# A twelve-stage transformer stack on one core: the quantised layers' fronts made in the drain of the stage before them, weights and cleared operands a stage sooner

## The reference, cut to what matters

```
x = x + 0.5 * L0_ffn(ln(x));  x = x + L0_attn(ln(x));  x = x + 0.5 * L0_ffn(ln(x))
x = x + 0.5 * L1_ffn(ln(x));  x = x + L1_attn(ln(x));  x = x + 0.5 * L1_ffn(ln(x))
... the same with L2 and L3
```

```
xn = layernorm(x) * ln_gamma + ln_beta
gamma = max(abs(xn))                       # over all 4096 tokens
xq = clip(xn * 128 / gamma, -128+, 128-);  y = (xq @ w_q) * gamma * beta / 128
```

## Time and profile before

| | before |
|---|---|
| median of 3 runs | 4267.09 us (4266.0 to 4274.78) |
| the profiled execution | 4268.37 us |
| its span, first to last instruction | 4266.6 us |
| mean granted TensorE clock | 0.951 |
| PE busy | 3884.7 us (91%) |
| DVE busy | 3266.5 us (77%) |
| ACT busy | 3119.9 us (73%) |
| POOL busy | 1511.8 us (35%) |

### The profile page before, as it was taken

How to read it: one execution, slowest core, us unless ns; L and a number is a source line. 1 busy time by engine, 2 the same in 40 slices (tenths; PEclk the granted TensorE clock), 3 DMA queues, 4 the chain that set the end, 5 groups by cost and what they waited for, 6 DMA issues and landing times.

```text
span 4266.6 us, 58145 instructions
## 1 busy us (share of the span) xinstructions
PE 3884.7 (91%) x15924; PEld 2177.6 (51%) x15924; DVE 3266.5 (77%) x10600; ACT 3119.9 (73%) x5775; POOL 1511.8 (35%) x2843
## 2 busy tenths in 40 slices
PE   6799789999999999999999999998699669999976
PEld 4567634444444444444444444443366447777755
DVE  6877588888888888888888888886667766666668
ACT  3555369999999999999999999998243436666654
POOL 2331234444444444444444444443211114333320
PEclk8888799999999999999999999999799879999988
DMA  2122010000000000000100000000000001111100
GB/s 61 31 45 40 7 25 1 15 11 1 20 6 1 20 6 1 20 6 1 23 3 8 18 1 16 11 1 1 0 1 1 0 15 46 46 45 43 43 7 20
DMA packets 151990, 71.08 MB, mean 17 GB/s; under 512 B 109577, under 2 KB 142685, under 8 KB 151667
## 3 DMA queue, kind: packets, MB, share of 16 engines
q1 hardware_dynamic: 144738, 63.96, 5.8%
q10 hardware_dynamic: 6928, 3.41, 0.3%
HBM read 54.55 MB, written 12.80 MB: 16 GB/s over the span
## 4 chain that ended last, share of the span: by engine, by line
PE 59%; ACT 18%; DVE 14%; issue 6%; POOL 3%; DMA 0%; DVEq 0%; SPq 0%; ACTq 0%; POOLq 0%
PE bank L2093 16%; PE bank L2883 5%; PE bank L2108 5%; PE bank L2137 5%; ACT arena L2185 3%; PE bank L2916 3%; PE bank L2147 3%; ACT arena L2184 2%; ACT arena L2188 2%; ACT arena L2197 2%; DVE arena L2274 2%; ACT L2231 2%; PE bank L620 2%; PE bank L2943 1%; DVE arena L2297 1%
## 5 line engine op out<-in xcount | busy, mean ns | idle before, releaser
L2093 PE MATMUL bank<-arena 128*128 128x512 f32 x3072 | 1413.5, 593 | 3.9 <-DMA arena<-in_L_attn_Wv_dram 3.7
L2093 PEld LDWEIGHTS bank<-arena 128*128 128x128 f32 x3072 | 584.0, 190 | 739.9 <-issue 719.3
L2334 POOL TENSOR_SCALAR arena<-arena 128x256 f32<-128x256 f32 x1024 | 481.1, 481 | 1156.3 <-DVE arena L2267 1156.3
L2108 PE MATMUL bank<-arena 128*128 128x512 f32 x1024 | 524.5, 604 | 49.6 <-DVE arena L2297 49.6
L2256 DVE SCALAR_TENSOR_TENSOR arena<-arena 128x256 f32<-128x256 f32 x1024 | 393.7, 421 | 184.9 <-ACT arena L2185 176.5
L2297 DVE SCALAR_TENSOR_TENSOR arena<-arena 128x256 f32<-128x256 f32 x1024 | 491.7, 524 | 13.6 <-issue 13.6
L2274 DVE SCALAR_TENSOR_TENSOR arena<-bank,bv,arena 128x256 f32<-128x256 f32 x1024 | 444.7, 472 | 0.0
L2184 ACT ACTIVATE arena<-bank,bqk 128x512 f32<-128x512 f32 x512 | 348.5, 681 | 76.8 <-PE bank L2093 72.5
L2267 DVE SCALAR_TENSOR_TENSOR arena<-bank,bq,arena 128x512 f32<-128x512 f32 x512 | 384.1, 750 | 18.0
L2197 ACT ACTIVATE arena<-arena,const_table 128x512 f32<-128x512 f32 x512 | 374.7, 732 | 0.0
L2188 ACT ACTIVATE arena<-bank,bqk 128x512 f32<-128x512 f32 x512 | 354.3, 692 | 0.4 <-PE bank L2093 0.4
(11 more groups left out here) (396 smaller groups left out, 7056.3 us busy)
## 6 DMA issues: line engine op xcount, KB each, us to landing
arena<-packed_dram SPq DMA_DIRECT2D x96, 96.0 KB
arena<-packed_dram SPq DMA_DIRECT2D x32, 288.0 KB
arena<-diag_dram SPq DMA_DIRECT2D x16, 256.0 KB, 3.7
arena<-in_L_attn_Wk_dram SPq DMA_DIRECT2D x16, 256.0 KB, 3.2
arena<-in_L_attn_Wq_dram SPq DMA_DIRECT2D x16, 256.0 KB, 4.0
arena<-in_L_attn_Wv_dram SPq DMA_DIRECT2D x16, 256.0 KB, 4.2
arena<-in_L_attn_Wo_dram SPq DMA_DIRECT2D x8, 512.0 KB, 4.1
arena<-in_L_attn_W_dram SPq DMA_DIRECT2D x16, 256.0 KB, 2.7
```

The lines of the kernel that those rows point to most:

```text
L2093: nc.tensor.matmul(bank[:, RING1[m % 5], :], w1p[k][:, i * P:(i + 1) * P], zT_of(g), start=True, stop=True).then_inc(a1_proj.sem, 1)
L2108: nc.tensor.matmul(bank[:, 6, :], wo1[:, i, :], a1_att[:, i % 4, :], start=(i == 0), stop=(i == NB1 - 1)).then_inc(a1_outd.sem, 1)
L2334: last = nc.gpsimd.tensor_scalar(a, a, 1.0, a1_ksum[:, i % 4, b:b + 1], ALU.add, ALU.mult)
```

## The change

- **The front of ffn1 after ffn0** (n = 3). In ffn0's drain DVE does stats of groups 0 to 3 and apply of groups 0 to 2 between its last adds, and PE transposes group 0. ACT's gate is taken away from `affine_act`, and `f1_all` no longer lies where ffn0's tensors are.
- **The end of attn1 and the front of ffn1 after it** (n = 5). The three loops at the end are gone. `fin_pool` and its copy are left out: `fin_pe` transposes `zT` directly, into three banks instead of two. `ending(...)` puts steps at a place of slot 8, 9 or 10 of the last layer: fin for groups 0 to 6, and all of the front (stats, rstd, apply, turn, affine, max) for groups 0 to 5, and for group 6 all but max. On DVE `drained_dve_0` stands before `norm_stats_dve(1)` of slot 8 and `drained_dve_1` behind it, `_2` and `_3` so in slot 9, `_4` and `_5` in slot 10. Only group 7 is left for after the drain. ffn1's transposes go to banks 5 and 7 there.
- **attn1's first weights**: the SP wait is for the stage before the one in front, so the loads are issued when ffn0 has ended and ffn1 begins. The weights change places in the arena with the six tensors a1_ek to a1_att, so that they don't lie in ffn1's.
- **attn0's seven memsets** go to the end of the POOL program of ffn0 (n = 0), without a wait, and their tensors to columns that ffn0 doesn't use.
- **attn3's memsets** go to the end of the POOL program of ffn2 (n = 8), with a wait for stage 7.

```diff
+            def closing_pe(left):
+                if into_ffn1 and left == 1:
+                    begin(n + 1, "turn", 0)
             def closing(left):
-                if left in (1, 2):
+                if into_ffn1:
+                    if left == 3:
+                        begin(n + 1, "stats", 0, 1)
+                    if left == 2:
+                        begin(n + 1, "apply", 0, 1)
+                        begin(n + 1, "stats", 2)
+                    if left == 1:
+                        begin(n + 1, "apply", 2)
+                        begin(n + 1, "stats", 3)
+                elif left in (1, 2):
                     begin_early(n, "stats" if left == 2 else "apply")
...
+            programs["gpsimd"].append(lambda e: [clear(e) for clear in clears.get(n + 1, ())])
...
+            turn_bank = (5, 7) if stages[n - 1] == "attn1" else (0, 1)
             def affine_act(g, u):
+                if g == 0 and stages[n - 1] == "attn1":
+                    a1_outd.wait(nc.scalar, NL1 * G - 1)
...
-            programs["scalar"].append(lambda e: over_groups(e, [(0, affine_act)], gate(e, n)))
+            programs["scalar"].append(lambda e: over_groups(e, [(0, affine_act)]))
...
-            def clear_pool():
-                x_written.wait(nc.gpsimd, n * G - 1)
+            def clear_pool(e):
+                if n > 1:
+                    x_written.wait(e, (n - 1) * G - 1)
...
-                if n:
-                    x_written.wait(sp, n * G - 1)
+                if n > 1:
+                    x_written.wait(sp, (n - 1) * G - 1)
...
+                def drained_dve_0():
+                    fin_dve(0)
+                    fin_dve(1)
+                    begin(n + 1, "stats", 0, 1)
+                    fin_dve(2)
+                    begin(n + 1, "apply", 0, 1)
+                def drained_dve_1():
+                    fin_dve(3)
+                    begin(n + 1, "stats", 2)
+                    fin_dve(4)
+                    begin(n + 1, "stats", 3)
+                    begin(n + 1, "apply", 2)
+                def drained_dve_2():
+                    begin(n + 1, "apply", 3)
+                    begin(n + 1, "stats", 4)
+                    fin_dve(5)
+                    begin(n + 1, "stats", 5)
+                    begin(n + 1, "max", 0, 1)
+                    begin(n + 1, "apply", 4, 5)
...
                     if w == 2:
+                        if layer == NL1 - 1:
+                            pe.append((G, ending(lambda: (fin_pe(0), fin_pe(1), fin_pe(2)),
+                                                 lambda: (begin(n + 1, "turn", 2), fin_pe(5)),
+                                                 lambda: fin_pe(6))))
                         pe.append((2, turn_back_pe(0)))
+                        if layer == NL1 - 1:
+                            pe.append((G, ending(lambda: None, lambda: begin(n + 1, "turn", 3))))
                     if w == 7:
+                        if layer == NL1 - 1:
+                            pe.append((G, ending(lambda: (fin_pe(3), begin(n + 1, "turn", 0, 1), fin_pe(4)),
+                                                 lambda: begin(n + 1, "turn", 4, 5),
+                                                 lambda: begin(n + 1, "turn", 6))))
                         pe += [(3, turn_back_pe(1)), (2, h2_pe(1))]
...
                     if w == 7:
+                        if layer == NL1 - 1:
+                            act.append((G, ending(lambda: None, lambda: begin(n + 1, "affine", 2, 3))))
                         act.append((3, back_act(1)))
+                        if layer == NL1 - 1:
+                            act.append((G, ending(lambda: begin(n + 1, "affine", 0, 1),
+                                                  lambda: begin(n + 1, "affine", 4, 5),
+                                                  lambda: begin(n + 1, "affine", 6))))
...
-            def fin_pool(g, u):
-                a1_f_turned.wait_free(nc.gpsimd, g)
-                nc.gpsimd.tensor_copy(a1_fin[:, u, :], zT_of(g)).then_inc(a1_f_copied.sem, 1)
...
-                over_groups(e, [(0, fin_pe)])
+                fin_pe(G - 1)
...
-                over_groups(e, [(0, fin_dve), (4, begin_next("stats")), (6, begin_next("apply"))])
+                fin_dve(G - 1)
...
-            def program_pool(e):
-                if n:
-                    x_written.wait(e, (n - 1) * G)
+            def clear_pool(e):
+                x_written.wait(e, (n - 2) * G - 1)
                 nc.gpsimd.memset(a3_v[:], 0.0).then_inc(a3_cleared, 1)
```

More of the change, by code:

```diff
@@ L253, in once, with begin @@
             return step
+        def begin(n, name, *groups):
+            for g in groups:
+                early[n, name](g, g % 2)
         def begin_early(n, name):
@@ L477, in ffn1, with transpose_pe @@
         def ffn1(n, rep):
-            stats_dve, rstd_pool, apply_dve, transpose_pe, _ = ln_steps(n, 1e-5, 1e-3)
+            stats_dve, rstd_pool, apply_dve, _, _ = ln_steps(n, 1e-5, 1e-3)
+            rstd_pool = once("rstd", n, rstd_pool)
+            turn_bank = (5, 7) if stages[n - 1] == "attn1" else (0, 1)
+            def transpose_pe(g, u):
+                ln_applied.wait(nc.tensor, g + n * G)
+                xt_ready.wait_free(nc.tensor, g + n * G)
+                for q in range(QT):
+                    last = nc.tensor.transpose(bank[:, turn_bank[u], q * P:(q + 1) * P], xn[:, u, q, :], ident)
+                last.then_inc(xt_psum.sem, 1)
             def affine_act(g, u):
+                if g == 0 and stages[n - 1] == "attn1":
+                    a1_outd.wait(nc.scalar, NL1 * G - 1)
                 xt_psum.wait(nc.scalar, g + n * G)
                 apart(nc.scalar)
-                nc.scalar.activation(f1_all[:, bass.ds(g * GT, GT)], bank[:, u, :], ACT.Identity,
+                nc.scalar.activation(f1_all[:, bass.ds(g * GT, GT)], bank[:, turn_bank[u], :], ACT.Identity,
                                      bias=gb1[:, 1:2], scale=gb1[:, 0:1]).then_inc(xt_ready.sem, 1)
@@ L490, in max_dve @@
                                         apply_absolute_value=True).then_inc(f1_maxed.sem, 1)
+            transpose_pe, affine_act, max_dve = (once("turn", n, transpose_pe), once("affine", n, affine_act),
+                                                 once("max", n, max_dve))
             def scale_dve(dve):
@@ L666, in ffn2 @@
             programs["gpsimd"].append(lambda e: over_groups(e, [(0, rstd_pool)]))
+            programs["gpsimd"].append(lambda e: [clear(e) for clear in clears.get(n + 2, ())])
             programs["tensor"].append(lambda e: over_groups(
@@ L2365, in norm_rstd_pool, with drained_dve_3, drained_dve_4, drained_dve_5 @@
                     return fn
+                def drained_dve_0():
[17 more added lines that the diff above has]
+                    begin(n + 1, "apply", 4, 5)
+                def drained_dve_3():
+                    begin(n + 1, "max", 2, 3)
+                def drained_dve_4():
+                    begin(n + 1, "max", 4, 5)
+                    fin_dve(6)
+                    begin(n + 1, "stats", 6)
+                def drained_dve_5():
+                    begin(n + 1, "apply", 6)
                 pe, act, dve, pool = [], [], [], []
@@ L2447, in fin_pe @@
+            def fin_pe(g):
+                if g == 0:
+                    for k in "kqv":
+                        a1_read[k].wait(nc.tensor, NL1 * G - 1)
+                a1_zt.wait(nc.tensor, (NL1 - 1) * G + g)
+                if g >= len(FIN_BANKS):
+                    x_written.wait(nc.tensor, n * G + g - len(FIN_BANKS))
                 for q in range(QT):
-                    last = nc.tensor.transpose(bank[:, 2 + u, q * P:(q + 1) * P], a1_fin[:, u, q * P:(q + 1) * P],
-                                               ident)
+                    last = nc.tensor.transpose(bank[:, FIN_BANKS[g % len(FIN_BANKS)], q * P:(q + 1) * P],
+                                               zT_of(g)[:, q * P:(q + 1) * P], ident)
@@ L2460, in program_pe, with ending @@
+            def ending(*slots):
+                return lambda d, u: slots[d]() if 0 <= d < len(slots) else None
             def program_pe(e):
```

75 lines of the change are left out of this document (45 added, 30 removed).

## The result

The changed kernel takes **4237.73 us** (median of four, 4230.49 to 4238.89); the kernel before, in the same rounds, 4267.74. The ratio is 0.9926, with a 95% interval of 0.9912 to 0.9939: 30 us less, outside the 0.2% that the measurement can tell. The profiled execution took 4238.89 us with a span of 4236.7, against 4266.6 before. A second measurement of the same kernel, experiment 10, gave 4236.65 and the same ratio, 0.9926. One of the eleven runs of experiment 9's kernel took 9099.73 us, over twice as long as any other, and is left out of its ratio.

The account below looks back on a forecast made before the run. The largest limit was attn1's end, where one group at a time walks through PE, DVE, POOL and ACT. Terms -24.2 - 2.9 - 2.8 - 4.4 + 0.6 = -33.7 us gave 4234.7, as a median 4233.4; range 4225 to 4247.

Parts of the forecast that it names:

- End of attn1: At attn1's end, only group 7 stays behind the drain; the scale comes 24.2 us sooner, bounds -28.7 and -19.3.
- the drain: In attn1's drain, gains and delays from the inserted work sum to 0.0 us, bounds -4.5 and +4.9.
- The new wait: In attn1's drain, slot 9, PE waits before turn 4 and 5 for ACT's affine: +2.1 us, bounds -1 and +2.9.
- 0.9 was taken: In attn1's drain, h2 of group 7 is 3.0 us late, of which PE's clock may give back 0.9.
- rival 2: In attn1's drain, PE's clock stays up and saves 8 us: 4225 us; chance 0.10.
- Front after ffn0: From ffn0's end, DVE passes move between adds that waited for PE: -2.9 us, bounds -3.7 and -1.5.
- First weights: At attn1's start, early loads let the first product start when ACT has written its input: -2.8 us, bounds -2.9 and -1.5.
- attn3's memsets: Moved from ffn3 to ffn2, they give DVE back 4.4 us and cost ffn2 nothing; bounds -4.8 and 0.
- attn0's memsets: Moved from attn0's start into ffn0, they return 0.2 us but delay an apply: net +0.6, bounds -0.2 and +2.5.
- each of its four instructions may wait for one memset: In ffn0, group 7's apply gets through as single memsets end, so PE starts at 50.3, +0.8 us.
- the dear bound: In ffn0, group 7's apply has its last instruction wait for all memsets, to 51.8 us: +2.7 us.

Follow-up runs that it names:

- experiment 10: The changed kernel measured once more, unaltered, against the kernel before; 4236.65 us, ratio 0.9926.
- experiment 9: The kernel before with only idle work added: 56 PE transposes, whose results nobody reads, in the drain of attn1's last layer; 4265.56 us, ratio 0.9998.
- experiments 5 and 6: Changed kernel with all parts but the end of attn1 undone, 4250.37 us; changed kernel with attn3's memsets back in ffn3, 4249.52 us; both ratios 0.9943.

## Why the prediction came out, step by step

**End of attn1: right, 2.7 us too small.** Forecast 24.2, measured 26.9 in six executions and 25.1 in two. Behind the drain 9.0 us were forecast and 8.8 came. The term that was mis-sized is the drain, "0.0, bounds -4.5 and +4.9": it measured -2.6 in six and -0.7 in two. The new wait came where it was put, 4.3 us long. Counted from the step at 2961.30 (2959.26 before), turn_back behind it began 37.9 us in, where it had been 38.3; the forecast's terms up to there add up to 0.6 us later. The clock gave back more than was priced: PE ran at 1.00 in the slots in front, where it had fallen to 0.79, and h2 of group 7 took 3.26 us instead of 5.13, 1.9 us back where 0.9 was taken. That is a part of rival 2. Experiment 9 supports that PE's extra work does it, in one execution. Rival 2's 8 us didn't come: of the six stretches of 8 us from 2959.26 on, before had one at full clock, four at 0.79 to 0.85 and one at 0.71, and in the changed drain the clock still fell at the end, to 0.79 and 0.91.

**Front after ffn0: right direction, 2.1 us for 2.9**, within its bounds, and the same in experiments 5 and 6. The last add of ffn0 is 1.5 us late behind apply 2 and stats 3, where 0.8 was taken.

**First weights: the mechanism is right, the sum isn't seen.** The product starts 2.7 us sooner behind its input, without a wait for the load. In executions of the same course that is worth 2.1 to 3.4 us, and 2.8 was forecast. In the two profiles compared, and so in the 29.9 us, they are worth nothing, because the changed kernel has falls of PE's clock in the first layer that before did not have. This the prediction did not foresee.

**attn3's memsets: right.** L831 and L836 are at 0.18 us, 4.4 us, and no pass in ffn2 is longer. Another 1.6 us came in this profile with PE's clock at ffn3's end. The passes over PSUM and over two tensors did not wait for POOL: L676 took 0.75 us and L680 0.75 under the memsets as elsewhere. The page "SBUF — State Buffer" of the Trainium skill (Who interferes with whom) says that a DVE instruction with at most one SBUF input, outside the two-port modes, does not contend with GpSimd; the 0.75 us of L676, whose source is in PSUM, agree.

**attn0's memsets: wrong in size.** Forecast +0.6 net with a bound of +2.5; the changed kernel's profiles show +4.3 and +3.0 in the first stretch. The step that failed is "each of its four instructions may wait for one memset". In three of five executions this is about what happened, at +0.6 to 0.8 against the 27.05 of before, with 0.33 to 0.35 us of wait of PE for the apply. In the stretch itself that can't be told, for it reaches 27.99 where no memset runs beside the apply. (The prediction's own ends of the passes give a start of PE at 50.1 and not 50.3, +0.6.) In the other two the passes waited to the end of the row, as the dear bound had it, at 2.7 us for the late start of PE. It measured 2.9 in both. In the second profile that is about all of the +3.0. In the first the products behind ran at half clock, which has no term in the sum: four transposes 1.12 us for 0.60, and a clock of 0.58 between 52 and 56 us, where the second had 1.00 between 51 and 55.

So 33.7 us were forecast and 29.9 came in the profiles. The parts that beat the forecast (end of attn1, 2.7; ffn3's end, 1.6) are less than those that fell short (memsets in ffn0, 3.7; the first layer with the weights, 2.9; the front, 0.8; the stretch behind ffn1's scale, 0.6): 4.3 against 8.0. That the whole came within 4 us of the forecast is thus in part luck: the misses cancel, and most of them go with a clock that changes from one execution to the next.

Two things stay open. Why a row of memsets lets DVE's passes in between in one execution and not in another, no run told apart: in all five executions the apply started 0.11 to 0.14 us behind the start of the second memset, and two of them had the long outcome. And what decides whether PE's clock falls behind a given wait, since the same code went both ways. Medians of kernels that differ by 2 to 4 us of real work are therefore not a verdict on that work here.

## What to carry to other kernels

Where one group at a time walks through the drain of a pipeline, put the next stage's work for the finished groups into its waits. Most of the gain here is this (24.3 us behind the drain, 0.7 to 2.6 in it, of 30), and the one wait that it added cost less than it looked. Here clears by GpSimd cost nothing to see where VectorE read PSUM or two tensors or waited for loads, and beside passes over one SBUF tensor they did little harm with a semaphore step between them. When a part is worth less than the stages that nobody touched vary by, cut the traces at common steps and judge that stretch, in several executions; two ratios of whole times could not have told the first weights (0.9926 and 0.9932), and one profile of each kernel called them worthless.

## What the runs showed of the hardware

- Seven memsets in a row without a pause held a four-instruction pass of VectorE for 6.14 and 6.17 us, and for 3.74 to 3.76 in three other executions. With a semaphore step between them it was 2.96, and the row took 8.12 us instead of 7.4 to 7.7.
- The same products behind the same wait of 2.75 us ran in 1.12 or in 2.08 us, as the granted clock stayed at 1.00 or was 0.63. In the one execution with extra transposes that nobody reads, a drain was 2.9 us shorter.
- Stretches of unchanged code took 410.4 to 416.2 us and 757.4 to 764.3 us from kernel to kernel. In attn1's first layer, its drain and ffn3's end PE's granted clock had fallen in the longer execution. Behind ffn3 the clock goes the same way: 0.948 to 0.953 in the seven executions of 757.4 to 757.9 us, 0.938 to 0.943 in the seven of 761.0 to 764.3. In attn0 it does not explain the length: 410.4 us at 0.834, and 414.0 and 416.2 at 0.835 and 0.832.
